# Attention: softmax inverses from a 128 by 16 layout, laid out and spread by transfers

## The chip, the cores and the metric

The kernel runs on one core of a Trainium2 chip. Its matrix engine (PE), vector engine (DVE), scalar engine (ACT) and general engine (POOL) each work through a program of their own and meet at semaphores; transfers are issued here by a fifth sequencer (SP). The metric is the time of one execution on the device in microseconds (us). Before the change the median of three runs is 5288.91 us.

## The reference

The program is one transformer block over x of shape (4, 2048, 512), in float32: a layer norm, then 16 heads of attention and a mixture of two experts beside each other, both added to x. What matters here is the attention:

```python
qkv = jnp.einsum('bnc,dc->bnd', x, qkv_w) + qkv_b
q, k, v = (qkv[0], qkv[1], qkv[2])        # each (4, 16 heads, 2048, 32)
attn = jnp.einsum('bhqd,bhkd->bhqk', q, k) * scale
attn = jax.nn.softmax(attn, axis=-1)
out = jnp.einsum('bhqk,bhkd->bhqd', attn, v)
...
x = x + _L0_attn_ref(xn, ...) + _L0_ffn_ref(xn, ...)
```

The softmax needs the largest score of each row, the exponentials, their sum, and a division by the sum. The kernel divides at the end: it multiplies the finished products of exponentials and values by the inverse of the sum.

## The kernel before

There are three stages one after the other: `dense_stage` (norm, projections, experts, to about 1,310 us of the profile), `attention_stage` (to 5,087 us) and `output_stage`. The change is in the second.

**Groups.** Attention is cut into 64 groups: 4 batches by 4 sets of four heads, each by 4 chunks of 512 queries. The four chunks of one set of heads share their keys and values. A group holds, for four heads and 512 queries, all 2048 keys. Eight groups (two sets of heads) make one turn of a loop; the first and the last turn are written out, six run in the loop.

**Units and scores.** PE computes each group's scores twice. The first time, one group ahead, it makes 64 *units* of 128 by 512 scores in three banks `mx_ps` (L890), and DVE takes the maxima of each (L829): unit n may only be written once the maxima of unit n-3 are taken. The second time (L951), with the maxima already folded in as one more row, the scores go to `st_ps`, and ACT takes the exponential into `p_sb` (L814). POOL adds the exponentials in pairs (L766, L756). PE multiplies them by the values (L902, sum in `o_ps`) and adds the pairs up with a matrix of ones (L910, sum in `sum_ps`). Those ones are 32 columns wide, so in `sum_ps` all 32 partitions of a head hold the same 512 sums.

**The order of the work** is written by hand. A group has 8 steps; the strings `STEPS` (L645) say what PE does in each: U is a unit, S a block of scores, V the products with the values, Z the sums, T the transposed maxima. Most steps read `USUSUSV...USUSUSUSUS`: three units, the products, then five more units. Of one step, `units_of(j)` lists the units, and DVE walks the same list (L861 to L873).

**The inverses.** They belong to the group before. In step 1 of a group ACT copies the finished sums of the group before to `sum_raw` (L792, 128 partitions by 512). DVE inverts them in 8 pieces of 64 columns (L843), two in each of the steps 2 to 5: one after the third unit of a step (i == 2), which is just ahead of V on PE, the other after the seventh (i == 6), in the middle of the run of units. In step 6 it multiplies (L849, `normalise`), and SP stores the result (L696).

**SP's order.** At the start of a set of heads (qc == 0) SP issues the transfers of the next set's keys (three of 1 MB, L675) and values (1 MB, L679), and then three of 256 KB of queries (L683). In the other groups it issues three of queries alone. After that it waits for the shift of step 6 and stores the group before. Keys and values of a next set are loaded at the heads of 15 sets; at the first of them there are no inverses yet, so 14 groups (the 4th, 8th, ... 56th, counted from 0) have both.

Of the kernel before, what the change touches and what calls it, by code (L numbers as in the profile page):

```python
# [15 lines left out]
F32 = mybir.dt.float32  # L16
# [6 lines left out]
P = 128  # L23
B, N, C = 4, 2048, 512
H, D = 16, 32
# [4 lines left out]
TOK = 512  # L30
# [542 lines left out]
                turn(B - 1, True)  # L573


def attention_stage(nc, qh_d, ql_d, kh_d, kl_d, v_d, o_d):

# [3 lines left out]
    QC = N // TOK  # L583
    UN = 4 * TT * (N // 512)
    NP = KT // 2
    INV = 8
    SLOTS = 8
    AHEAD = 6
    SB = 3
# [10 lines left out]
    with ctx:  # L600
        def sb(name, shape, dt):
            return ctx.enter_context(nc.sbuf_tensor(name, shape, dt))

        def sem(name):
            return ctx.enter_context(nc.semaphore(name))
# [11 lines left out]
        o_raw = sb("o_raw", [P, TOK], F32)  # L617
        sum_raw = sb("sum_raw", [P, TOK], F32)
        o_inv = sb("o_inv", [P, TOK], F32)
        st_ps = [ctx.enter_context(nc.psum_tensor(f"st_ps{i}", [P, TOK], F32)) for i in range(SB)]  # L620
        mx_ps = [ctx.enter_context(nc.psum_tensor(f"mx_ps{i}", [P, 512], F32)) for i in range(3)]
        o_ps = ctx.enter_context(nc.psum_tensor("o_ps", [P, TOK], F32))
# [10 lines left out]
        exp_done, o_copied, sum_copied, shift_done = sem("exp_done"), sem("o_copied"), sem("sum_copied"), sem("shift_done")  # L633
        unit_done, max_done, inv_done, o_done = sem("unit_done"), sem("max_done"), sem("inv_done"), sem("o_done")
        pair_done = sem("pair_done")

        G = 2 * QC
        TURNS = NQ // 2
# [30 lines left out]
        with nc.Block() as block:  # L669

            @block.sync
            def _(sp):
# [13 lines left out]
                def load_shift(count, qc):  # L686
# [2 lines left out]
                    sp.dma_start(q_x[qc][R:R + 1, :, :].bitcast(F32),  # L689
                                 shift[:, :].bitcast(F32)).then_inc(shift_ld, 16)  # L690

                def store_group(turn0, it, qc, count):
                    dst = o_d[it, :, qc * TOK:(qc + 1) * TOK]
                    sp.lower_val(dst.offset * 4)
                    sp.wait_ge(o_done, count)
                    sp.dma_start(dst, o_inv[:, :]).then_inc(o_st, 16)  # L696
# [11 lines left out]
                def turn(L, first, last):  # L708
                    for g in range(G):
                        u, qc = g // QC, g % QC  # L710
                        it, more = L * 2 + u, not (last and u == 1)
                        if qc == 0 and more:

                            sp.wait_ge(pv_done, L * G * KT + g * KT)
                            load_keys(it + 1 if isinstance(it, int) else it + 1, 1 - u)
                            load_values(it + 1, 1 - u)
                        if qc > 0 and more:

                            sp.wait_ge(st_ready, L * G * SK + g * SK)
                            load_queries(it + 1, qc - 1)  # L720
                        if qc == 0 and not (first and u == 0):
                            sp.wait_ge(st_ready, L * G * SK + g * SK)
                            load_queries(it, QC - 1)
                        if not (last and g == G - 1):
                            load_shift(L * G + g + 2, (qc + 1) % QC)
                        if not (first and g == 0):
                            store_group(L, it - 1 if qc == 0 else it, (qc - 1) % QC, L * G + g)

                turn(0, True, False)
                with sp.Fori(1, TURNS - 1) as L:  # L730
                    turn(L, False, False)
                turn(TURNS - 1, False, True)
                store_group(0, NQ - 1, QC - 1, NQ * QC)
                sp.wait_ge(o_st, NQ * QC * 16)

# [38 lines left out]
            def _(act):  # L774
# [13 lines left out]
                def copy_sum(count):  # L788

                    act.wait_ge(sum_done, count * NS)  # L790
                    act.wait_ge(inv_done, (count - 1) * INV)
                    act.activation(sum_raw[:, :], sum_ps[:, :], ACT.Copy).then_inc(sum_copied, 1)  # L792

                turn_shift(1)
# [30 lines left out]
            def _(dve):  # L825
# [8 lines left out]
                    dve.wait_ge(rows_ready, count - 1)  # L834
                    dve.reduce_max(row_max[:, :], unit_max[:, :, :], AX.X).then_inc(max_done, 1)

                def invert(count, part):

                    cols = slice(part * TOK // INV, (part + 1) * TOK // INV)
                    if part == 0:  # L840
                        dve.wait_ge(sum_copied, count)
                        dve.wait_ge(o_st, (count - 1) * 16)
                    dve.reciprocal(o_inv[:, cols], sum_raw[:, cols]).then_inc(inv_done, 1)  # L843

                def normalise(count):

                    dve.wait_ge(inv_done, count * INV)
                    dve.wait_ge(o_copied, count)
                    dve.tensor_tensor(o_inv[:, :], o_raw[:, :], o_inv[:, :], ALU.mult).then_inc(o_done, 1)  # L849

# [8 lines left out]
                def turn(L, first, last):  # L859
                    for g in range(G):  # L860
                        for j in range(NP):  # L861
# [3 lines left out]
                            for i, n in enumerate(units_of(j)):  # L865
                                if not (last and g + ahead >= G):
                                    if n == 0:
                                        dve.wait_ge(max_done, L * G + g + 2)
                                    unit((L * G + g + ahead) * UN, n)
                                if 2 <= j < 6 and i in (2, 6) and not (first and g == 0):  # L870
                                    invert(L * G + g, 2 * (j - 2) + (i == 6))
                            if j == AHEAD - 1 and not (last and g + ahead >= G):
                                rows((L * G + g + ahead) * UN, L * G + g + 2)  # L873

# [1 line left out]
                with dve.Fori(1, TURNS - 1) as L:  # L876
                    turn(L, False, False)
                turn(TURNS - 1, False, True)
                for part in range(INV):
                    invert(NQ * QC, part)  # L880
                normalise(NQ * QC)

            @block.tensor
# [253 lines left out]
def block_kernel(nc, x, qkv_wT, qk_bT, v_b, proj_wT, proj_b, wr, br, w1, b1T, w2, b2, out):  # L1137
# [8 lines left out]
    xf = x.rearrange("b n c -> (b n) c")  # L1146
    of = out.rearrange("b n c -> (b n) c")
    dense_stage(nc, xf, x0, qkv_wT, qk_bT, v_b, wr, br, w1, b1T, w2, b2, proj_b, qh_d, ql_d, kh_d, kl_d, v_d, y_d)
    attention_stage(nc, qh_d, ql_d, kh_d, kl_d, v_d, o_d)
    output_stage(nc, proj_wT, o_d, y_d, of)  # L1150


# [28 lines left out]
```

## Time and profile before

| what | us |
|---|---|
| median of 3 runs (5285.81 to 5292.80) | 5288.91 |
| the profiled execution | 5284.76 |
| its span | 5281.8 |
| PE busy (matmuls) | 5093.4 |
| DVE busy | 3277.4 |
| ACT busy | 2587.7 |
| POOL busy | 3229.5 |
| reciprocals of 64 columns (L843), 512 of them | 276.2 |
| maxima (L829), 4096 of them | 2503.2 |

The span is the time between the first and the last instruction; the 3.0 us around it are start and end. Ends of matmuls are modelled, so PE counts as busy where it waits for less than the modelled length of its last matmul: its waits are better read from the distance between starts. The rows further down are from the views of this one profiled execution. Group 28 (counted from 0) stands for a group at the head of a set of heads inside the loop's turn, group 32 for one at the head of the turn.

### The profile page before, as it was taken

To read this page: it belongs to the slowest core of one execution; us is meant where nothing else is said; L and a number is where in the kernel's file an instruction comes from. 1 tells how busy PE (TensorE), PEld (TensorE's weight loads), DVE (VectorE), ACT (ScalarE), POOL (GpSimd) and SP (SyncE) were. 2 spreads that over 40 slices of the span, in tenths; PEclk is the share of its full clock that TensorE was granted. 3 is DMA by queue.
4 is the path that set the end of the run, shared out by engine and by line. 5 is a ranking of instruction groups with operands and counts; after the bars stand their busy time and mean duration, and the time that the engine had idled before them with its cause. 6 is when DMAs were issued, how large, how long until landed. Compare 5 with 4: busy or idle time off the path is not lost. (4 is left out here: it accounts for less than half of the span.)

```text
span 5281.8 us, 83204 instructions
## 1 busy us (share of the span) xinstructions
PE 5093.4 (96%) x25932; PEld 2867.8 (54%) x25932; DVE 3277.4 (62%) x5616; ACT 2587.7 (49%) x4717; POOL 3229.5 (61%) x861
## 2 busy tenths in 40 slices
PE   8999999999899999999999999999999999999979
PEld 6878878787444444444444444444444444444447
DVE  4232232331777777777777777777777777777724
ACT  2121121211366666666656666665666566666631
POOL 1212212122488788778877877887788778778830
PEclk9999999999799999999999999999999999999989
DMA  5343343432402112120202202020220202020047
GB/s 172 91 150 105 99 148 94 140 119 77 95 17 51 28 44 49 25 49 17 51 23 50 49 20 55 17 50 18 55 49 19 55 17 49 19 55 17 7 154 240
DMA packets 186069, 348.49 MB, mean 66 GB/s; under 512 B 17956, under 2 KB 51748, under 8 KB 177448
## 3 DMA queue, kind: packets, MB, share of 16 engines
q1 hardware_dynamic: 185640, 342.99, 23.2%
q8 instruction: 242, 3.96, 0.3%
q14 instruction: 187, 1.53, 0.1%
HBM read 208.19 MB, written 134.22 MB: 65 GB/s over the span
## 5 line engine op out<-in xcount | busy, mean ns | idle before, releaser
L829 DVE TENSOR_REDUCE unit_max<-mx_ps 128x1 f32<-128x512 f32 x4096 | 2503.2, 679 | 918.4 <-PE mx_ps L890 918.4
L766 POOL TENSOR_TENSOR p_pair<-p_sb 128x2048 f32<-128x2048 f32 x512 | 2366.0, 4637 | 781.2 <-PE sum_ps L910 418.3
L814 ACT ACTIVATE p_sb<-st_ps 128x512 f32<-128x512 f32 x4096 | 2212.9, 600 | 1041.4 <-PE st_ps L951 1031.2
L890 PE MATMUL mx_ps<-k_x,q_x 96*128 96x512 f32 x4096 | 1853.6, 461 | 100.6 <-DVE unit_max L829 49.4
L951 PE MATMUL st_ps<-q_x,k_x 97*128 97x512 f32 x4096 | 1629.2, 403 | 8.2 <-ACT p_sb L814 2.3
L890 PEld LDWEIGHTS mx_ps<-k_x,q_x 96*128 96x128 f32 x4096 | 767.5, 190 | 1162.6 <-DVE unit_max L829 836.9
L902 PE MATMUL o_ps<-p_sb,v_sb 128*32 128x512 f32 x8192 | 992.5, 602 | 0.0
L951 PEld LDWEIGHTS st_ps<-q_x,k_x 97*128 97x128 f32 x4096 | 777.6, 190 | 137.1 <-ACT p_sb L814 64.6
L756 POOL TENSOR_TENSOR p_pair<-p_pair 128x2048 f32<-128x2048 f32 x128 | 584.6, 4567 | 10.0
L285 POOL TENSOR_TENSOR h_lo<-h_f,h_hi 128x512 fp32r<-128x512 f32 x128 | 165.1, 1290 | 689.8 <-DVE h_hi L469 689.8
L902 PEld LDWEIGHTS o_ps<-p_sb,v_sb 128*32 128x32 f32 x8192 | 214.6, 109 | 490.8 <-issue 278.9
L342 ACT ACTIVATE h_f<-rot,b_sb 128x512 f32<-128x512 f32 x128 | 88.2, 689 | 644.5 <-PE rot L505 644.4
L910 PE MATMUL sum_ps<-p_pair,ones 128*32 128x512 f32 x3072 | 388.8, 593 | 4.8 <-POOL p_pair L766 4.7
L469 DVE CAST h_hi<-h_f 128x512 fp32r<-128x512 f32 x128 | 55.0, 431 | 542.2 <-ACT h_f L342 542.2
L843 DVE RECIPROCAL o_inv<-sum_raw 128x64 f32<-128x64 f32 x512 | 276.2, 542 | 66.5 <-ACT sum_raw L792 66.5
L326 ACT ACTIVATE qk_hi<-rot,qk_bias 128x512 fp32r<-128x512 f32 x128 | 88.1, 689 | 379.2 <-DMA q_lo_d<-qk_lo 167.2
L910 PEld LDWEIGHTS sum_ps<-p_pair,ones 128*32 128x32 f32 x3072 | 99.8, 110 | 237.8 <-issue 215.6
L503 PE MATMUL rot<-xnT_hi,wq_hi 128*128 128x512 f32 x512 | 202.1, 395 | 19.5 <-DVE qk_lo L433 11.4
L503 PE MATMUL acc<-we_hi,h_hi 128*128 128x512 f32 x512 | 206.1, 402 | 6.5 <-POOL h_lo L285 4.9
L503 PE MATMUL rot<-xnT_hi,we_hi 128*128 128x512 f32 x512 | 199.6, 390 | 1.6 <-DVE v_out L455 1.6
L504 PE MATMUL rot<-xnT_lo,wq_hi 128*128 128x512 f32 x512 | 201.1, 393 | 0.0
L505 PE MATMUL rot<-xnT_hi,wq_lo 128*128 128x512 f32 x512 | 201.1, 393 | 0.0
(92 smaller groups left out, 3513.4 us busy)
## 6 DMA issues: line engine op xcount, KB each, us to landing
q_x<-q_hi_d SPq DMA_DIRECT2D x128, 256.0 KB, 5.4
k_x<-k_hi_d SPq DMA_DIRECT2D x30, 1024.0 KB, 9.6
xt<-x SPq DMA_DIRECT2D x64, 256.0 KB, 2.7
stage<-w SPq DMA_DIRECT2D x32, 512.0 KB, 5.1
q_hi_d<-qk_hi SPq DMA_DIRECT2D x64, 256.0 KB, 3.0
q_lo_d<-qk_lo SPq DMA_DIRECT2D x64, 256.0 KB, 3.7
k_hi_d<-qk_hi SPq DMA_DIRECT2D x64, 256.0 KB, 2.6
k_lo_d<-qk_lo SPq DMA_DIRECT2D x64, 256.0 KB, 3.3
```

The costliest lines, as they stand in the source:

```text
L503: pe.matmul(out, lh, rh, start=start and k == 0, stop=False)
L504: pe.matmul(out, lh, rl, start=False, stop=False)
L505: op = pe.matmul(out, ll, rh, start=False, stop=stop and k == len(pairs) - 1)
L756: pool.tensor_tensor(p_pair[:, slot, :, :], p_pair[:, 0, :, :], p_pair[:, slot, :, :], ALU.add).then_inc(pair_done, 1)
L766: pool.tensor_tensor(p_pair[:, slot, :, :], p_sb[:, 2 * i % SLOTS, :, :], p_sb[:, (2 * i + 1) % SLOTS, :, :], ALU.add).then_inc(pair_done, 1)
L814: act.activation(p_sb[:, kt % SLOTS, h, :], st_ps[bank(g, m)][:, :], ACT.Exp, scale=SCALE).then_inc(exp_done, 1)
L829: dve.reduce_max(unit_max[:, n // 4, n % 4:n % 4 + 1], mx_ps[n % 3][:, :], AX.X).then_inc(unit_done, 1)
L843: dve.reciprocal(o_inv[:, cols], sum_raw[:, cols]).then_inc(inv_done, 1)
L890: pe.matmul(mx_ps[n % 3][:, :], q_x[qc][0:R, h, t * P:(t + 1) * P], k_x[u][0:R, h, kc * 512:(kc + 1) * 512], start=True, stop=True).then_i ...
L902: op = pe.matmul(o_ps[rows, :], v_sb[u][:, kt, rows], p_sb[:, kt % SLOTS, h, :], start=(kt == 0), stop=(kt == KT - 1))
L910: op = pe.matmul(sum_ps[h * D:(h + 1) * D, :], ones[:, :], p_pair[:, slot, h, :], start=(i == 0), stop=(i == NS - 1))
L951: pe.matmul(st_ps[bank(g, m)][:, :], k_x[u][:, h, kt * P:(kt + 1) * P], q_x[qc][:, h, :], start=True, stop=True).then_inc(st_ready, 1)
```

## The change

The sums are inverted in another shape. Since 32 partitions hold the same values, SP now takes one partition of each head, 4 by 512 sums, and lays them out as 128 partitions by 16 columns in `sum_t` (one transfer of 8 KB). DVE inverts that in one instruction, in step 3 after the third unit. SP writes the inverses to a scratch tensor `inv_d` in memory (8 KB), waits until they have landed, and reads them back with four transfers that copy each head's 512 inverses to its 32 partitions of `o_inv` (64 KB each). `normalise` is where it was and now waits for the four transfers. ACT's next copy of sums waits for the first transfer instead of for the reciprocals.

```diff
+                def spread_inverse(count):
+                    sp.wait_ge(sum_copied, count)
+                    sp.dma_start(sum_t[:, :], sum_raw[0:P:D, :]).then_inc(sum_ld, 16)
+                    sp.wait_ge(inv_done, count)
+                    sp.dma_start(inv_d.rearrange("h (r n) -> (h r) n", n=QR), inv_t[:, :]).then_inc(inv_st, 16)
+                    sp.wait_ge(inv_st, count * 16)
+                    if not (isinstance(count, int) and count == 1):
+                        sp.wait_ge(o_st, (count - 1) * 16)
+                    for h in range(4):
+                        sp.dma_start(o_inv[h * D:(h + 1) * D, :], inv_d[h, :].partition_broadcast(D)).then_inc(inv_ld, 16)
...
                         if qc == 0 and not (first and u == 0):
                             sp.wait_ge(st_ready, L * G * SK + g * SK)
                             load_queries(it, QC - 1)
+                        if not (first and g == 0):
+                            spread_inverse(L * G + g)
                         if not (last and g == G - 1):
                             load_shift(L * G + g + 2, (qc + 1) % QC)
...
                 turn(TURNS - 1, False, True)
+                spread_inverse(NQ * QC)
                 store_group(0, NQ - 1, QC - 1, NQ * QC)
...
-                    act.wait_ge(inv_done, (count - 1) * INV)
+                    if not (isinstance(count, int) and count == 1):
+                        act.wait_ge(sum_ld, (count - 1) * 16)
...
-                def invert(count, part):
-                    cols = slice(part * TOK // INV, (part + 1) * TOK // INV)
-                    if part == 0:
-                        dve.wait_ge(sum_copied, count)
-                        dve.wait_ge(o_st, (count - 1) * 16)
-                    dve.reciprocal(o_inv[:, cols], sum_raw[:, cols]).then_inc(inv_done, 1)
+                def invert(count):
+                    dve.wait_ge(sum_ld, count * 16)
+                    if not (isinstance(count, int) and count == 1):
+                        dve.wait_ge(inv_st, (count - 1) * 16)
+                    dve.reciprocal(inv_t[:, :], sum_t[:, :]).then_inc(inv_done, 1)
...
-                    dve.wait_ge(inv_done, count * INV)
+                    dve.wait_ge(inv_ld, count * 64)
...
-                                if 2 <= j < 6 and i in (2, 6) and not (first and g == 0):
-                                    invert(L * G + g, 2 * (j - 2) + (i == 6))
+                                if j == 3 and i == 2 and not (first and g == 0):
+                                    invert(L * G + g)
```

On DVE, the first group that has inverses (group 1) read like this before, from the maxima ahead of the first reciprocal to those of the row maxima:

```order
L829 TENSOR_REDUCE unit_max<-mx_ps 128x1 x33
L843 RECIPROCAL o_inv<-sum_raw 128x64
L829 TENSOR_REDUCE unit_max<-mx_ps 128x1 x4
L843 RECIPROCAL o_inv<-sum_raw 128x64
L829 TENSOR_REDUCE unit_max<-mx_ps 128x1 x4
L843 RECIPROCAL o_inv<-sum_raw 128x64
L829 TENSOR_REDUCE unit_max<-mx_ps 128x1 x4
L843 RECIPROCAL o_inv<-sum_raw 128x64
L829 TENSOR_REDUCE unit_max<-mx_ps 128x1 x4
```

Each group now has one reciprocal among its 64 maxima:

```order
L848 TENSOR_REDUCE unit_max<-mx_ps 128x1 x41
L861 RECIPROCAL inv_t<-sum_t 128x16
L848 TENSOR_REDUCE unit_max<-mx_ps 128x1 x23
L854 TENSOR_REDUCE row_max<-unit_max 128x16
L867 TENSOR_TENSOR o_inv<-o_raw,o_inv 128x512
```

It stands where the third of the eight stood; the other seven are gone. On SP, at the head of the second set of heads of the first turn (group 4), the order before is keys, values, queries, shift, store:

```order
L675 DMA k_x<-k_hi_d 32x4x2048 x2
L675 DMA k_x<-k_lo_d 32x4x2048
L679 DMA v_sb<-v_d 128x2048
L683 DMA q_x<-q_hi_d 32x4x512
L683 DMA q_x<-q_lo_d 32x4x512
L683 DMA q_x<-q_hi_d 32x4x512
L689 DMA q_x<-shift 1x16x128
L696 DMA o_d<-o_inv 128x512
```

Now the six new transfers stand between the queries and the shift, the first of them behind the 4.75 MB of keys, values and queries:

```order
L678 DMA k_x<-k_hi_d 32x4x2048 x2
L678 DMA k_x<-k_lo_d 32x4x2048
L682 DMA v_sb<-v_d 128x2048
L686 DMA q_x<-q_hi_d 32x4x512
L686 DMA q_x<-q_lo_d 32x4x512
L686 DMA q_x<-q_hi_d 32x4x512
L698 DMA sum_t<-sum_raw 128x1x16
L700 DMA inv_d<-inv_t 128x16
L705 DMA o_inv<-inv_d 32x512 x4
L692 DMA q_x<-shift 1x16x128
L711 DMA o_d<-o_inv 128x512
```

## Rows read from the trace of the kernel before

**Rows 1.** The page, engines: busy us (share of the span), instructions.

```profile
PE 5093.4 (96%) x25932; PEld 2867.8 (54%) x25932; DVE 3277.4 (62%) x5616; ACT 2587.7 (49%) x4717; POOL 3229.5 (61%) x861
```

**Rows 2.** Waits of PE between 1480 and 5010 us: total, times, longest.

```profile
PE mx_ps L890 <- DVE unit_max L829: 48.6, 183, 0.3
```

**Rows 3.** Group of instructions, 1480 to 5010 us: busy us, mean ns, idle before.

```profile
L829 DVE TENSOR_REDUCE unit_max<-mx_ps 128x1 f32<-128x512 f32 x3904 | 2386.5, 679 | 877.7 <-PE mx_ps L890 877.7
```

**Rows 4.** Timeline of PE, products with values, group 0: start us, us.

```profile
1395.12 1.92 PE L902 MATMUL o_ps<-p_sb,v_sb 128*32 128x512 f32 x16
1401.31 1.92 PE L902 MATMUL o_ps<-p_sb,v_sb 128*32 128x512 f32 x16
1407.51 1.92 PE L902 MATMUL o_ps<-p_sb,v_sb 128*32 128x512 f32 x16
1415.15 1.92 PE L902 MATMUL o_ps<-p_sb,v_sb 128*32 128x512 f32 x16
```

**Rows 5.** The same four of group 1.

```profile
1451.35 1.92 PE L902 MATMUL o_ps<-p_sb,v_sb 128*32 128x512 f32 x16
1457.95 1.92 PE L902 MATMUL o_ps<-p_sb,v_sb 128*32 128x512 f32 x16
1464.55 1.92 PE L902 MATMUL o_ps<-p_sb,v_sb 128*32 128x512 f32 x16
1472.60 1.92 PE L902 MATMUL o_ps<-p_sb,v_sb 128*32 128x512 f32 x16
```

**Rows 6.** Timeline of PE, units of group 28 around a reciprocal.

```profile
3015.90 0.50 PE L890 MATMUL mx_ps<-k_x,q_x 96*128 96x512 f32 x1
...
3016.90 0.50 PE L890 MATMUL mx_ps<-k_x,q_x 96*128 96x512 f32 x1 [0.27 <-DVE unit_max L829]
```

**Rows 7.** Timeline of DVE, group 28, steps 2 and 3.

```profile
3015.76 0.54 DVE L843 RECIPROCAL o_inv<-sum_raw 128x64 f32<-128x64 f32 x1
3016.22 2.42 DVE L829 TENSOR_REDUCE unit_max<-mx_ps 128x1 f32<-128x512 f32 x4
3018.55 0.54 DVE L843 RECIPROCAL o_inv<-sum_raw 128x64 f32<-128x64 f32 x1
3019.96 2.48 DVE L829 TENSOR_REDUCE unit_max<-mx_ps 128x1 f32<-128x512 f32 x4 [0.86 <-PE mx_ps L890]
```

**Rows 8.** Timelines of group 28: ACT's copy of the sums, SP's last queries.

```profile
3006.83 0.60 ACT L792 ACTIVATE sum_raw<-sum_ps 128x512 f32<-128x512 f32 x1 [2.22 <-PE sum_ps L910]
3002.10 0.38 SPq L683 DMA_DIRECT2D q_x<-q_hi_d  x1
```

**Rows 9.** Transfers issued 3001.9 to 3002.6 us: count, KB, us to landing.

```profile
q_x<-q_hi_d SPq DMA_DIRECT2D x1, 256.0 KB, 21.4
```

**Rows 10.** Group 32: last queries' issue, their us to landing, DVE's maxima.

```profile
3236.68 0.38 SPq L683 DMA_DIRECT2D q_x<-q_hi_d  x1
q_x<-q_hi_d SPq DMA_DIRECT2D x1, 256.0 KB, 19.8
3254.46 2.48 DVE L829 TENSOR_REDUCE unit_max<-mx_ps 128x1 f32<-128x512 f32 x4 [0.86 <-PE mx_ps L890]
```

**Rows 11.** The page, transfers: count, KB, median us to landing.

```profile
q_x<-q_hi_d SPq DMA_DIRECT2D x128, 256.0 KB, 5.4
```

**Rows 12.** All transfers, small and near ones: count, KB, us to landing.

```profile
o_d<-o_inv SPq DMA_DIRECT2D x64, 256.0 KB, 2.5
q_x<-shift SPq DMA_DIRECT2D x64, 8.0 KB, 1.8
b_sb<-b1T SPq DMA_DIRECT2D x8, 2.0 KB, 1.6
```

**Rows 13.** Windows of group 28: length, busy by engine, PEclk, DMA share, GB/s.

```profile
3021.00:3023.00 2.00, 2.00 (x9) 1.04 (x7) 2.00 (x5) 2.00 (x5) 2.00 (x1) 1.00 0.16 43
```

**Rows 14.** The end of attention: DVE's timeline.

```profile
5080.04 3.43 DVE L843 RECIPROCAL o_inv<-sum_raw 128x64 f32<-128x64 f32 x8 [42.84 <-ACT sum_raw L792]
5083.51 0.69 DVE L849 TENSOR_TENSOR o_inv<-o_raw,o_inv 128x512 f32<-128x512 f32 x1
```

More of the change, by code:

```diff
@@ L573, in _, with attention_stage @@
                 turn(B - 1, True)
-def attention_stage(nc, qh_d, ql_d, kh_d, kl_d, v_d, o_d):
+def attention_stage(nc, qh_d, ql_d, kh_d, kl_d, v_d, inv_d, o_d):
     R = 3 * D
@@ L585, in attention_stage @@
     NP = KT // 2
-    INV = 8
+    QR = 4 * TOK // P
     SLOTS = 8
@@ L619, in attention_stage @@
         o_inv = sb("o_inv", [P, TOK], F32)
+        sum_t = sb("sum_t", [P, QR], F32)
+        inv_t = sb("inv_t", [P, QR], F32)
         st_ps = [ctx.enter_context(nc.psum_tensor(f"st_ps{i}", [P, TOK], F32)) for i in range(SB)]
@@ L635, in attention_stage @@
         pair_done = sem("pair_done")
+        sum_ld, inv_st, inv_ld = sem("sum_ld"), sem("inv_st"), sem("inv_ld")
         G = 2 * QC
@@ L878, in _ @@
                 turn(TURNS - 1, False, True)
-                for part in range(INV):
-                    invert(NQ * QC, part)
+                invert(NQ * QC)
                 normalise(NQ * QC)
@@ L1148, in block_kernel @@
     dense_stage(nc, xf, x0, qkv_wT, qk_bT, v_b, wr, br, w1, b1T, w2, b2, proj_b, qh_d, ql_d, kh_d, kl_d, v_d, y_d)
-    attention_stage(nc, qh_d, ql_d, kh_d, kl_d, v_d, o_d)
+    inv_d = scratch("inv_d", (4, TOK))
+    attention_stage(nc, qh_d, ql_d, kh_d, kl_d, v_d, inv_d, o_d)
     output_stage(nc, proj_wT, o_d, y_d, of)
```

## The prediction

> **What bounds the kernel now.** I read the page first: PE is busy for 96% of the span, DVE for 62% [rows 1]. By that alone, work taken off DVE would be worth nothing. The waits of PE in the middle of attention say otherwise: 183 times PE was idle before a unit until DVE had taken a maximum, 0.27 us or a little less each, and 183 is three times the 61 groups of that stretch [rows 2]. So something on DVE reaches PE three times a group. The timelines show what. Among the maxima DVE sits at a pace of 0.60 us ((2.48 - 0.68) / 3, with the 0.68 us of one maximum [rows 3, 7]), and PE's units follow DVE's pace there, since only three banks lie between them. Where a reciprocal comes in the middle of the run (3015.76), the next maximum starts 0.46 us later, and PE's units, at 3015.90 and 3016.90, stand 1.00 us apart instead of 0.60 [rows 6, 7]: PE loses 0.40 us. Where a reciprocal comes just ahead of the products with the values (3018.55), DVE waits another 0.86 us for PE after it [rows 7]: this one is hidden under products that keep PE 1.92 us [rows 4].
>
> The kernel has its own control. In group 0 there are no inverses yet. Its products of steps 2 to 5 start 6.19, 6.20 and 7.64 us apart; those of group 1, with two reciprocals a step, 6.60, 6.60 and 8.05 us [rows 4, 5]. That is 20.03 us against 21.25: 1.22 us per group, in three portions of 0.4 us. It fits the three waits a group; the fourth reciprocal of that kind, in step 5, has only two units left behind it and costs nothing.
>
> **The change, part by part.** *The eight reciprocals go.* Groups 1 to 62 have units beside their inverses (group 63 has none left), so this gives back 62 x 1.22 = 75.6 us. The other half of the reciprocals gives nothing. The 0.46 us a maximum that DVE loses behind one of 64 columns bounds the new one of 16 columns between 0.1 (a quarter of it) and 0.46 us; I take 0.2, since most of it scales with columns: eight in a row take 3.43 us [rows 14], 0.42 each for 64 columns. It stands ahead of the products, under the same 0.86 us, and costs nothing by itself. POOL and ACT do the same as before.
>
> *A wait of DVE on a transfer comes in.* Behind it in DVE's program stand all further maxima, and PE stops three units later. How late can the sums land? In most groups early: ACT's copy ends 0.60 us after 3006.83 [rows 8], and a small transfer takes 1.6 to 1.8 us, one of 256 KB out of the chip's own memory 2.5 [rows 12]; landed by about 3010, with DVE there at 3018.1. In those groups the chain behind it also fits: reciprocal, 2 us to memory, 1.3 us to issue four transfers, 2 us back, some 6 us, ahead of a multiplication twenty microseconds after 3018; SP has nothing else to issue until then.
>
> At the 14 heads of sets with keys and values it is different. The three transfers of queries are issued behind 4 MB of them: the last, issued at 3002.10, lands 21.4 us later, at 3023.5, where the median of such a transfer is 5.4 [rows 8, 9, 11]. So they stood in line, and the new transfer, issued at about 3007.5, joins the line behind them. DVE is free 0.41 us earlier than before (one portion of 0.4 is saved ahead of it), and would go on with maxima at 3019.96 - 0.41 = 3019.55 [rows 7]. With the sums at 3023.5, 0.1 us to wake and 0.2 for the reciprocal it goes on at 3023.8: 4.26 us late. In group 32, at the head of a turn, the last queries land at 3236.68 + 19.84 = 3256.5, and DVE would go on at 3254.46 - 0.41 = 3254.05 [rows 10]: 3256.52 + 0.3 is 2.77 us later. The 14 are seven of each kind, which differ little among themselves: 7 x 4.26 + 7 x 2.77 = 49.2 us. All of it reaches PE, as the run that follows goes at DVE's pace and nothing in later steps is slack enough to win it back.
>
> The transfer's own share comes on top, behind the last queries. Bounds: as much as 1.6 to 2.5 us, a whole small transfer end to end [rows 12], if nothing of it overlaps; or less than nothing. From 3021 to 3023 the 16 DMA engines are busy for a share of 0.16, two or three of them, with the rest of the queries [rows 13]: if the sums travel only on engines that are done, they land 1.4 us before 3023.5, which in the seven groups of that kind would make 10 us less. I take 0.5 us: 7.0 us for the 14, 56.2 in all.
>
> The Trainium skill has a rule on just this (DMA: Bandwidth & Descriptors, "Why a DMA increments its semaphore by 16 and not by 1"): a transfer is split over the largest number of engines up to 16 that divides the slowest dimension of both sides. By it the sums, 4 rows on one side, would go over 4 engines with 32 pieces each, and not over 16. No row of before shows a transfer of that shape. By this rule the late engines of a group like 28 need not be among the four; if they are not, the 10 us above come off and a profiled run takes 5260, and if they are, each has four times the pieces and the share is nearer to the upper bound. The first lies in the forecast's own range below, the second leads to the rival of a later landing.
>
> *The end.* After the last group nothing covers the chain. Before, the multiplication starts 3.47 us after the copied sums (5080.04 to 5083.51 [rows 14]). Now: 2.0 for the sums to land, 0.2 for the reciprocal, 2.0 to memory, 1.3 until the fourth transfer is issued, 2.2 to its landing, 0.3 for wakes: 8.0 us. That is 4.5 us more on the path, with 3 and 6.5 as bounds if each of the three legs takes 1.6 or 2.5 us [rows 12].
>
> *Sum*: -75.6 + 56.2 + 4.5 = -14.9 us. The profiled execution took 5284.8 us (span 5281.8 and 3.0 around it), so a profiled one should take 5270; the median of the runs is 4.1 us above the profiled one, so I forecast 5274 us for it, 0.28% faster. Most of what DVE gives back is lost again in 14 of 62 groups.
>
> **The rivals.** *The small transfer overtakes.* If it is served beside the big ones instead of behind them, DVE never waits in the heads: -75.6 + 4.5 = -71 us, 5218. For it speaks that pieces of 64 bytes are tiny; against it the queries, themselves a sixteenth of what is ahead, that waited 20 us.
>
> *The sums land later than that, and the kernel gets slower.* Break-even is where 14 delays eat 71.1 us: 5.08 us each, against the 4.0 I have on average. It decides from 1.1 us more. The mechanism would be the transfer's own latency at the end of the line: if 2.5 us and not 0.5 lie between the landing of the last queries and that of the sums [rows 12], the delays cost 28 us more and the time is 5302. For it: the pieces are small and many, and both ends lie in the chip's own memory, a pair of ends that the rows before never show. Against: the queries ahead, issued 0.4 us apart, do not each add a whole latency.
>
> *The reciprocals were never paid for*, and the two groups differ for another reason (group 0 also has no copies of sums on ACT). Then -75.6 is nothing and DVE's stalls remain: 5289 + 56 + 4.5 = 5349. The three waits a group stand against it.
>
> **How the numbers follow.** The forecast, with its own range of 5260 to 5288 (delays between 3.0 and 5.0 us), gets 0.62; overtaking or much of it 0.14; later landing 0.21; unpaid reciprocals 0.03. What a measurement of this kernel can tell from no change is about 0.2%, 10.6 us, so faster means below 5278.3 and slower above 5299.5. Of the forecast's 0.62, 0.40 lies below 5278 and 0.22 within; overtaking is all faster; of the later landing 0.06 is within and 0.15 slower; the last is slower. Faster 0.54, same 0.28, slower 0.18. The range of 8 in 10 takes in the later landing but not all of the overtaking: 5248 to 5303.
>
> **What would show it.** In the profile after: 62 groups without the three waits; products of steps 2 to 5 at 6.2, 6.2 and 7.65 us in ordinary groups; in 14 groups one distance of 6.2 plus 3 to 5 us between the products of steps 3 and 4, with DVE's reciprocal at the end of that wait and the sums' transfer landing 15 to 17 us after its issue instead of 2; the multiplication at the end some 8 us after the copy. Wrong would be: reciprocals in the heads that start at once, a landing over 2 us behind the last queries, or distances that stay at 6.6 us.

## The result, and the profile after

| | us |
|---|---|
| after, median of 4 runs (5320.62 to 5332.74) | 5328.92 |
| before, in the same rounds (5285.81 to 5292.80) | 5289.35 |
| ratio, 95% interval | 1.0073, 1.0055 to 1.0090 |
| profiled execution, after (before 5284.76) | 5330.07 |
| its span (before 5281.8) | 5327.6 |
| its mean granted clock of PE (before 0.987) | 0.971 |

The change makes the kernel 0.73% slower. The forecast was 5274 us with a range of 5248 to 5303: direction and range were wrong.

Look first at what got better, the engines' row of the page after (busy us, share, instructions):

```profile
PE 5137.1 (96%) x25932; PEld 2902.8 (54%) x25932; DVE 3205.5 (60%) x5168; ACT 2586.7 (49%) x4717; POOL 3221.3 (60%) x861
```

Against [rows 1], DVE lost 72 us of work, and PE, with the same 25932 instructions, is busy 44 us longer. Longer matmuls of the same number mean a lower clock. The waits between 1480 and 5050 us (total, times, longest) tell where that begins:

```profile
DVE inv_t L861 <- DMA sum_t<-sum_raw: 60.5, 14, 5.4
PE mx_ps L907 <- DVE unit_max L848: 49.6, 28, 3.8
```

The 183 waits of a quarter of a microsecond [rows 2] are gone, as forecast. In their place stand 14 waits of DVE on the sums, 4.3 us each, one in each of the 14 heads of sets, and 28 waits of PE: two per head, where the forecast has one. (The 4.0 us of the forecast are another quantity, the delay of DVE's next maximum. It comes below.)

To see what each head costs, take the distances between the products with the values (L919 after). Group 1, an ordinary one (start us, us of one):

```profile
1451.76 1.93 PE L919 MATMUL o_ps<-p_sb,v_sb 128*32 128x512 f32 x16
1457.94 1.93 PE L919 MATMUL o_ps<-p_sb,v_sb 128*32 128x512 f32 x16
1464.13 1.92 PE L919 MATMUL o_ps<-p_sb,v_sb 128*32 128x512 f32 x16
1471.78 1.92 PE L919 MATMUL o_ps<-p_sb,v_sb 128*32 128x512 f32 x16
```

6.18, 6.19 and 7.65 us instead of 6.60, 6.60 and 8.05 [rows 5]: the 1.22 us a group are there. Group 28, a head, steps 3 to 6:

```profile
3034.72 1.92 PE L919 MATMUL o_ps<-p_sb,v_sb 128*32 128x512 f32 x16
3045.39 2.54 PE L919 MATMUL o_ps<-p_sb,v_sb 128*32 128x512 f32 x16
3053.65 1.92 PE L919 MATMUL o_ps<-p_sb,v_sb 128*32 128x512 f32 x16
3059.84 1.93 PE L919 MATMUL o_ps<-p_sb,v_sb 128*32 128x512 f32 x16
```

The first distance is 10.67 us instead of 6.19, 4.5 us more, close to what was forecast. But the next is 8.26 instead of 7.65, and the matmuls of the second row take 2.54 instead of 1.92 us. Adding these distances over all groups and setting them against those of before gives the ledger:

| part | after minus before, us |
|---|---|
| 42 ordinary groups, 1.22 each | -51.2 |
| 14 heads, the same gain, 1.22 each | -17.1 |
| 14 heads, from the products of step 3 to those of step 4 (where the wait is) | +62.5 |
| 14 heads, steps 4 to 5 | +11.6 |
| 14 heads, steps 6 to 7 and 7 to the next group | +40.8 |
| the 6 other groups with inverses | -5.7 |
| end of attention | +5.1 |
| start and last stage | -0.4 |
| sum (the spans differ by 45.8) | +45.6 |

So behind the step of the wait the heads cost another 52.3 us, 3.7 each (the aftermath), and that alone turns the sign. How it comes about can be followed in group 28. DVE's and PE's timelines at the end of the wait:

```profile
3039.97 0.25 DVE L861 RECIPROCAL inv_t<-sum_t 128x16 f32<-128x16 f32 x1 [4.17 <-DMA sum_t<-sum_raw]
3040.14 3.06 DVE L848 TENSOR_REDUCE unit_max<-mx_ps 128x1 f32<-128x512 f32 x5
```

```profile
3040.82 0.80 PE L907 MATMUL mx_ps<-k_x,q_x 96*128 96x512 f32 x1 [2.57 <-DVE unit_max L848]
...
3065.31 0.50 PE L907 MATMUL mx_ps<-k_x,q_x 96*128 96x512 f32 x1 [0.83 <-DVE unit_max L848]
```

PE stood for 2.57 us and starts again with a unit of 0.80 us where 0.50 is usual: its clock has fallen. The windows of the group (length, busy by engine, granted clock, DMA share, GB/s) show it fall twice:

```profile
3034.70:3039.90 5.20, 3.55 (x23) 1.48 (x22) 1.10 (x2) 2.40 (x5) 5.12 (x2) 1.00 0.84 201
3039.90:3046.70 6.80, 5.88 (x18) 3.54 (x22) 5.31 (x9) 2.98 (x5) 5.87 (x2) 0.50 0.12 42
3046.70:3067.20 20.50, 19.37 (x104) 8.38 (x96) 16.59 (x22) 11.70 (x22) 15.66 (x5) 1.00 0.04 14
3067.20:3074.00 6.80, 6.80 (x26) 2.66 (x30) 2.95 (x5) 1.79 (x3) 4.18 (x1) 0.50 0.01 2
```

After the stop PE runs for 6.8 us at 1.2 GHz, then 20.5 us at 2.4 GHz, then 6.8 us more at 1.2 GHz. Over attention from 1480 to 5050 us there are 32 such stretches after: one at each of five loop back edges, 14 behind the waits, and in 13 heads a second one in step 6. Before there are 6: those of the back edges and one in group 62.

The first slow stretch begins at 3039.90, ahead of the products at 3045.39, so a part of the 62.5 us is slow clock and not wait. How much can be read from DVE. In group 1, whose products of step 3 start at 1457.94, it waits for PE before the next maximum although no transfer holds it:

```profile
1460.34 3.08 DVE L848 TENSOR_REDUCE unit_max<-mx_ps 128x1 f32<-128x512 f32 x5 [1.15 <-PE mx_ps L907]
```

This maximum starts 2.40 us behind the products of step 3; in group 28 it is 5.42 us (3034.72 to 3040.14). The delay is thus 3.0 us and not the 4.17 us of the wait: about 1.2 us of each wait lie where DVE would have waited for PE anyway. Over the 14 heads the delays make 44.4 us. The other 18 us of the 62.5 go with the slow stretch; e3 below has five heads without one, and there the step is longer by the delay alone.

Between the two slow stretches stands PE's other wait, of 0.83 us, and DVE and POOL tell what it is (DVE, then POOL):

```profile
3059.90 4.76 DVE L867 TENSOR_TENSOR o_inv<-o_raw,o_inv 128x512 f32<-128x512 f32 x1
3064.58 4.88 DVE L848 TENSOR_REDUCE unit_max<-mx_ps 128x1 f32<-128x512 f32 x8
```

```profile
3059.52 4.59 POOL L784 TENSOR_TENSOR p_pair<-p_sb 128x2048 f32<-128x2048 f32 x1 [1.95 <-ACT p_sb L833]
```

The multiplication, 0.69 us of work [rows 14], takes 4.76 us and ends 0.55 us after POOL's addition does. In an ordinary group it starts 2.7 us behind the start of an addition, and in the kernel before 4.1 to 4.4 us behind, when little of the 4.6 us is left. Here the stop and the slow stretch have moved it so late that it meets the next addition, which has also moved (POOL's own wait of 1.95 us on ACT) but less, and begins 0.38 us ahead of it. The maxima queued behind the multiplication are late, PE stops, and the clock falls again. Over all 64 groups (shortest, mean, longest, ns):

```profile
L867 DVE TENSOR_TENSOR o_inv<-o_raw,o_inv x64: 693/2435/4757, 1478.0 to 5130.1; 128x512 f32<-128x512 f32 x64
```

It is 2.4 us in most ordinary groups, where PE never waits for it, and 4.67 to 4.76 in each of the 14 heads. In both kernels 63 of the 64 multiplications start beside an addition, and each of them ends 0.55 or 0.56 us after that addition. Before, it took about 0.75 us in most groups:

```profile
3038.89 0.75 DVE L849 TENSOR_TENSOR o_inv<-o_raw,o_inv 128x512 f32<-128x512 f32 x1
```

The Trainium skill (SBUF — State Buffer, "Who interferes with whom") says that a DVE instruction with two inputs in SBUF, the on-chip memory, contends with a POOL instruction that reads SBUF, and that the shared ports are an exclusive lock. This trace agrees: 0.69 us of work took 4.76 us beside an addition of 4.59 us.

The end of attention after, SP's issues and DVE:

```profile
5123.21 0.58 SPq L698 DMA_DIRECT2D sum_t<-sum_raw  x1
...
5125.35 0.35 SPq L700 DMA_DIRECT2D inv_d<-inv_t  x1
...
5126.79 1.71 SPq L705 DMA_DIRECT2D o_inv<-inv_d  x4
```

```profile
5125.07 0.25 DVE L861 RECIPROCAL inv_t<-sum_t 128x16 f32<-128x16 f32 x1 [40.23 <-DMA sum_t<-sum_raw]
...
5130.08 0.69 DVE L867 TENSOR_TENSOR o_inv<-o_raw,o_inv 128x512 f32<-128x512 f32 x1 [4.75 <-DMA o_inv<-inv_d]
```

The copy of the sums ends at 5123.18. The multiplication starts 6.9 us later, against 3.47 [rows 14]: 3.4 us more where 4.5 were forecast. With nothing else on the queue the sums take 1.86 us from issue to reciprocal; in the heads 14.7 to 16.2.

### The profile page after: what moved, and what is told of

It reads as the page before. It is cut to its first block and busy times, and to the rows that moved or that the text cites. A ratio compares the mean times of both kernels' runs of the same rounds, so it can differ in the third digit from the quotient of the medians.

```text
span 5327.6 us, 83255 instructions
## 1 busy us (share of the span) xinstructions
PE 5137.1 (96%) x25932; PEld 2902.8 (54%) x25932; DVE 3205.5 (60%) x5168; ACT 2586.7 (49%) x4717; POOL 3221.3 (60%) x861
## 5 line engine op out<-in xcount | busy, mean ns | idle before, releaser
L907 PE MATMUL mx_ps<-k_x,q_x 96*128 96x512 f32 x4096 | 1875.0, 466 | 101.9 <-DVE unit_max L848 49.6
L968 PE MATMUL st_ps<-q_x,k_x 97*128 97x512 f32 x4096 | 1654.1, 409 | 8.4 <-ACT p_sb L833 2.3
L907 PEld LDWEIGHTS mx_ps<-k_x,q_x 96*128 96x128 f32 x4096 | 780.3, 193 | 1136.7 <-DVE unit_max L848 805.6
L919 PE MATMUL o_ps<-p_sb,v_sb 128*32 128x512 f32 x8192 | 1017.5, 615 | 0.0
L968 PEld LDWEIGHTS st_ps<-q_x,k_x 97*128 97x128 f32 x4096 | 791.9, 194 | 143.7 <-ACT p_sb L833 66.0
L919 PEld LDWEIGHTS o_ps<-p_sb,v_sb 128*32 128x32 f32 x8192 | 218.1, 111 | 513.8 <-ACT p_sb L833 273.6
L505 PE MATMUL acc<-we_hi,h_lo 128*128 128x512 f32 x512 | 200.6, 392 | 0.0
```

The source lines that it names most:

```text
L505: op = pe.matmul(out, ll, rh, start=False, stop=stop and k == len(pairs) - 1)
L907: pe.matmul(mx_ps[n % 3][:, :], q_x[qc][0:R, h, t * P:(t + 1) * P], k_x[u][0:R, h, kc * 512:(kc + 1) * 512], start=True, stop=True).then_i ...
L919: op = pe.matmul(o_ps[rows, :], v_sb[u][:, kt, rows], p_sb[:, kt % SLOTS, h, :], start=(kt == 0), stop=(kt == KT - 1))
L968: pe.matmul(st_ps[bank(g, m)][:, :], k_x[u][:, h, kt * P:(kt + 1) * P], q_x[qc][:, h, :], start=True, stop=True).then_inc(st_ready, 1)
```

## The experiments

The theory: in the heads the sums land late behind 4.75 MB, DVE stops, and PE pays for the stop three times (the stop, the slow stretch behind it, the multiplication locked behind POOL with a slow stretch of its own). The rivals: the reciprocals were never worth 75.6 us; or the transfers themselves disturb PE, DVE or POOL; or the 52 us belong to something else in the heads. Ratios are against the kernel before in the same rounds (5288.22 us in those of e1 to e4, 5298.48 us in those of e5 to e8, so times of the two sets are to be compared by ratio). "Excess" is the 14 heads' distances above 56.15 us, an ordinary group without reciprocals in the way.

### e1_four_pieces: the gain without the transfers

From the kernel before: four reciprocals of 128 columns, each just ahead of the products.

```diff
-    INV = 8
+    INV = 4
...
-                                if 2 <= j < 6 and i in (2, 6) and not (first and g == 0):
-                                    invert(L * G + g, 2 * (j - 2) + (i == 6))
+                                if 2 <= j < 6 and i == 2 and not (first and g == 0):
+                                    invert(L * G + g, j - 2)
```

> The kernel before, with four reciprocals of 128 columns instead of eight of 64, all in the place that was hidden (after the third unit of steps 2 to 5), none in the middle of a run of units. No transfers are added. Theory (the three mid-run reciprocals are what DVE's time was worth, and the lower clock of the changed kernel comes from its stalls): products of steps 2 to 5 at 6.2, 6.2, 7.65 us, 62 x 1.22 = 76 us less, 5213 us, and no more stretches at the lower clock than the kernel before has (11). Rival (a denser PE by itself makes the clock fall, as it fell in the changed kernel): stretches at 1.2 GHz in the heads of sets here too, and 5230 to 5265 us.

Measured: 5212.41 us, ratio 0.9851 (0.9834 to 0.9867), no excess. Among PE's own waits from 1480 to 5050 us none on DVE's maxima is left. DVE at the last reciprocal and the multiplication of group 27:

```profile
2945.03 0.94 DVE L843 RECIPROCAL o_inv<-sum_raw 128x128 f32<-128x128 f32 x1
2946.43 3.68 DVE L829 TENSOR_REDUCE unit_max<-mx_ps 128x1 f32<-128x512 f32 x6 [0.46 <-PE mx_ps L890]
2950.32 2.41 DVE L849 TENSOR_TENSOR o_inv<-o_raw,o_inv 128x512 f32<-128x512 f32 x1
```

After a reciprocal of 0.94 us DVE still waits 0.46 us for PE: it is hidden whole. The 75.6 us were real, and they came from the place of the reciprocals in the middle of the run of units (three of the four there, by the waits of [rows 2]), not from the work. This is the best version of all, faster than both kernels. It also shows that a multiplication of 2.4 us by itself costs nothing.

### e2_one_step_later: the same transfers, the reciprocal in step 4

```diff
-                                if j == 3 and i == 2 and not (first and g == 0):
+                                if j == 4 and i == 2 and not (first and g == 0):
```

> The changed kernel with one number different: the reciprocal stands after the third unit of step 4 instead of step 3, 7.6 to 8 us later. In the changed kernel the sums came 3.7 to 5.4 us too late in 14 groups. Theory (the wait in the 14 heads and what follows from it is the whole loss of 115 us): no wait on the sums anywhere, all ordinary and head groups at 56.2 us, 5329 - 115 = 5214, some 5217 us. Rival (the six transfers a group, their traffic and SP's longer program cost something by themselves): above 5235 us without such waits.

Measured: 5215.22 us, ratio 0.9856 (0.9839 to 0.9872). DVE waits for the sums in no head, the excess is 0, and of the slow stretches those at the five loop back edges are left, none in a head. All transfers are as in the changed kernel, so nothing of its loss belongs to them as such: all of it comes from DVE meeting the late sums. It is 2.8 us behind e1; that can't be told from nothing by these intervals, though the end's 3.4 us would be about it.

### e3_sum_on_act_queue: out of the line

ACT issues the sums' transfer from a queue of its own; SP keeps the rest.

```diff
-                    sp.wait_ge(sum_copied, count)
-                    sp.dma_start(sum_t[:, :], sum_raw[0:P:D, :]).then_inc(sum_ld, 16)
...
                     act.activation(sum_raw[:, :], sum_ps[:, :], ACT.Copy).then_inc(sum_copied, 1)
+                    act.wait_ge(sum_copied, count)
+                    act.dma_start(sum_t[:, :], sum_raw[0:P:D, :]).then_inc(sum_ld, 16)
```

> The changed kernel, with the transfer of the sums issued by ACT, on ACT's queue, right behind its copy; everything else stays on SP's. Theory (the sums are late because they stand behind the bulk in one queue): on a queue of their own they land in 2 to 5 us in the heads too, DVE does not wait, 5215 to 5230 us. Rival (the DMA engines are busy and any transfer started then is late): landing 15 us after its issue in the heads, waits of DVE as before, near 5329 us.

Measured: 5312.24 us, ratio 1.0039 (1.0025 to 1.0053), nearest to the rival's 5329, and as the rival had it, DVE got the sums 14.3 to 15.3 us after their issue. The excess is 84.4 us: 45.7 from step 3 to 4, 36.2 behind it, and 2.5 in step 1, where ACT now issues a transfer. DVE's waits:

```profile
DVE inv_t L861 <- DMA sum_t<-sum_raw: 52.3, 14, 4.3
```

3.7 us each instead of 4.3. So "the small transfer stands in line behind the big ones" is not the whole cause: it has hardly anything to gain from a line of its own. The page's row of that queue (packets, MB, share) and ACT's issue in the head shown:

```profile
q10 hardware_dynamic: 8448, 0.53, 0.1%
```

```profile
3022.85 0.56 ACTq L811 DMA_DIRECT2D sum_t<-sum_raw  x1
```

8448 packets for 64 transfers are 132 each: 128 pieces of 64 bytes and 4 packets of 4 bytes. The four fit the split over 4 engines that the forecast worked out; the records don't name a packet's engine. In this head the transfer was issued at 3022.85, and its pieces went out from 3029.6 to 3036.6 us, a few at a time, while the big transfers still ran (the last queries landed at 3038.4). DVE got them at last:

```profile
3037.68 0.25 DVE L861 RECIPROCAL inv_t<-sum_t 128x16 f32<-128x16 f32 x1 [3.84 <-DMA sum_t<-sum_raw]
```

So half of the 14.8 us pass while the pieces move. That they take turns with bulk packets is the likely reading, and e8 tests it; the 6.8 us until the first one moves are not explained by any run.

This run also parts the lock from the clock. In nine heads a slow stretch follows the wait. In the other five (groups 20, 24, 28, 44, 48) none does, and there the step of the wait is 2.06 to 2.64 us longer, with delays of DVE's next maximum of 2.11 to 2.69 us. Group 28: window, multiplication, PE's second wait.

```profile
3037.70:3063.00 25.30, 23.38 (x118) 10.40 (x119) 21.76 (x31) 14.56 (x27) 21.85 (x6) 1.00 0.08 23
```

```profile
3055.49 4.75 DVE L867 TENSOR_TENSOR o_inv<-o_raw,o_inv 128x512 f32<-128x512 f32 x1
```

```profile
3060.89 0.50 PE L907 MATMUL mx_ps<-k_x,q_x 96*128 96x512 f32 x1 [0.80 <-DVE unit_max L848]
```

The multiplication is locked all the same, at a granted clock of 1.00, so a shift of 2.1 us is enough for the lock and no slow stretch is needed. PE's second stop of 0.8 us costs 1.19 to 1.23 us in these five heads, and the clock doesn't fall behind it.

### e8_act_queue_64_pieces: half the pieces

As e3, with the sums laid out on 64 partitions by 32 columns.

```diff
-    QR = 4 * TOK // P
+    QR = 4 * TOK // 64
...
-        sum_t = sb("sum_t", [P, QR], F32)
-        inv_t = sb("inv_t", [P, QR], F32)
+        sum_t = sb("sum_t", [64, QR], F32)
+        inv_t = sb("inv_t", [64, QR], F32)
```

> As the run with the sums on ACT's queue (5312 us), but the sums laid on 64 partitions by 32 columns: 64 pieces of 128 bytes instead of 128 of 64. In that run the pieces of ACT's queue went out between 3029.5 and 3036.5, about one for each packet of the bulk on their four engines, and DVE waited 3.8 us. Theory (queues take turns piece by piece, so the number of pieces sets the landing): the pieces need half as long, 3.5 us less, DVE waits 0 to 0.6 us, 5215 to 5235 us. Rival (the sums land when the bulk is done, whatever their number): waits of 3 to 4 us as before, 5312 us.

Measured: 5227.33 us, ratio 0.9869 (0.9852 to 0.9886).

```profile
DVE inv_t L861 <- DMA sum_t<-sum_raw: 22.0, 14, 2.4
```

```profile
q10 hardware_dynamic: 4352, 0.53, 0.1%
```

```profile
2993.95 0.34 DVE L861 RECIPROCAL inv_t<-sum_t 64x32 f32<-64x32 f32 x1 [2.38 <-DMA sum_t<-sum_raw]
```

68 packets a transfer instead of 132, and the wait falls from 3.7 to 1.6 us: the pieces matter, though less than in proportion (in the head shown they go out in 5.6 us instead of 7). The time is in the expected range, but the wait was expected to be 0 to 0.6 us. More telling is what these waits cost. 22 us of them, the longest 2.4, make an excess of only 8.6 us: no slow stretch follows any, and in no head does the multiplication take over 2.4 us. Of the excess 6.3 us lie in the step of the wait, so about 1.1 us of each wait are absorbed ((22.0 - 6.3) / 14), as in the kernel after, and the other 2.3 come from ACT's issue in step 1 (it adds some 0.14 us to each ordinary group too). The price per microsecond of wait is not constant.

### e4_no_multiplication: the second stop taken out

The kernel after, with a short reduction of one operand in place of the multiplication. It leaves out the normalisation, so its output is wrong and it serves for the timing alone.

```diff
-                    dve.tensor_tensor(o_inv[:, :], o_raw[:, :], o_inv[:, :], ALU.mult).then_inc(o_done, 1)
+                    dve.reduce_max(o_inv[:, 0:1], o_raw[:, 0:64], AX.X).then_inc(o_done, 1)
```

> The changed kernel, but DVE's multiplication of 128 by 512 (two inputs) is left out and a maximum over 64 columns (one input) stands in its place, with the same waits; the output is not normalised. In the changed kernel the multiplication takes 2.4 us in ordinary groups and 4.7 in heads instead of 0.75, as long as POOL's addition beside it still runs. Theory: that lock is a part of the loss: in the 14 heads the step behind it (27 us of excess in all) shrinks by 10 to 25 us, 5305 to 5320 us. Rival (that excess is the clock alone, falling again after the first stall): heads as before, 5329 us.

Measured: 5287.18 us, ratio 0.9996 (0.9986 to 1.0005). The waits of DVE and PE:

```profile
DVE inv_t L861 <- DMA sum_t<-sum_raw: 62.6, 14, 5.2
...
PE mx_ps L907 <- DVE unit_max L848: 40.4, 14, 3.6
```

DVE waits as long as ever, but PE stops 14 times and not 28, and no second slow stretch is left (19: five of the back edges, 14 behind the waits). The excess is 77.3 us: 61.8 in the step of the wait, 15.2 from step 4 to 5, nothing in steps 6 and 7, where the kernel after loses 40.8. In ordinary groups the multiplication costs nothing either way, so those 40.8 us are what it brings when it meets POOL's addition in a head. The run is 42 us faster than the kernel after, where 10 to 25 had been expected: the second slow stretch goes with the lock. By e3's price of 1.2 us a head the lock itself is some 17 of the 40.8 us and the second stretch some 24.

### e5_long_hold: a stop without any transfer

From e1: in the same 14 heads, in step 3, DVE executes eight extra reciprocals of 64 columns, each waiting for the one before, into a tensor nobody reads.

```diff
+                                    if j == 3 and g % 4 == 0 and not (last and g == 4):
+                                        for m in range(8):
+                                            if not (first and m == 0):
+                                                dve.wait_ge(held, L * 16 + (g // 4 - 1) * 8 + m)
+                                            dve.reciprocal(hold[:, :], sum_raw[:, 0:64]).then_inc(held, 1)
```

> The version with four hidden reciprocals (5212 us), and in the 14 heads DVE is held at the place of the changed kernel's wait (step 3, after the third unit) by eight more reciprocals of 64 columns, each waiting for the last, into a tile that nobody reads: some 4 to 4.5 us beyond what is hidden. No new transfers. Theory (a stop of DVE of that length is enough for the whole loss: PE at 1.2 GHz behind it, then the multiplication locked behind POOL's addition, then 1.2 GHz again): heads 7 to 8.5 us longer, 5212 + 105 to 120, near 5322 us. Rival (the aftermath belongs to the transfers that were in flight): only the hold itself, 5212 + 14 x 4.2 = 5271 us.

Measured: 5341.24 us, ratio 1.0080 (1.0062 to 1.0097). DVE in group 4:

```profile
1628.15 4.60 DVE L878 RECIPROCAL hold<-sum_raw 128x64 f32<-128x64 f32 x8
...
1652.70 4.67 DVE L851 TENSOR_TENSOR o_inv<-o_raw,o_inv 128x512 f32<-128x512 f32 x1
```

```profile
PE mx_ps L897 <- DVE unit_max L831: 60.9, 28, 3.5
```

PE's 28 waits are back, with no transfer of sums in the kernel. The excess is 129.8 us: 75.2 in the step of the hold (5.4 each, of which the delay of DVE's next maximum is 4.0 and the rest goes with the slow clock) and 54.6 behind it (12.5, 27.0 and 15.0 in the segments where the kernel after has 11.6, 27.1 and 13.7). The same aftermath from another cause of such a stop: it belongs to the stop, not to transfers.

### e6_short_hold: half the stop

The same with four reciprocals (`range(4)`, 2.25 us in all).

> The same with four held reciprocals instead of eight: about 2 us beyond what is hidden. If the aftermath is an answer to the length of PE's stop, little of it remains: 14 x 2 = 28 us, 5240 us. If any stop in that place brings the same aftermath (3.7 us a head), 5212 + 28 + 52 = 5292 us. If the lock of the multiplication depends on how far the two engines' phases have been shifted, a value between, with the multiplication at 2.4 to 4.7 us.

Measured: 5271.04 us, ratio 0.9954 (0.9940 to 0.9967); excess 62.8 us, 28.8 in the step of the hold and 34.0 behind it. This divides the heads, though PE's stop is the same in all 14 (1.16 to 1.19 us) and so is the delay of DVE's next maximum (1.6 us). In eight heads the clock falls behind the hold, their step is 2.06 to 2.82 us longer, and the multiplication is locked. In the other six it doesn't fall and the step is 1.53 to 1.58 us longer; in five of these (groups 8, 32, 36, 40, 48) nothing follows, and in group 24 the multiplication is locked even so and the clock falls behind that. The nine heads with a lock pay the 34.0 us, 3.8 each, as much as in e5. PE's waits number 23, 14 and 9 more:

```profile
PE mx_ps L897 <- DVE unit_max L831: 24.5, 23, 1.5
```

The multiplication of a head whose clock fell behind the hold (28), of one whose clock never fell (32), and of group 24, DVE's rows and POOL's beside them:

```profile
3041.67 4.70 DVE L851 TENSOR_TENSOR o_inv<-o_raw,o_inv 128x512 f32<-128x512 f32 x1
...
3277.33 0.85 DVE L851 TENSOR_TENSOR o_inv<-o_raw,o_inv 128x512 f32<-128x512 f32 x1
...
2809.80 5.38 DVE L851 TENSOR_TENSOR o_inv<-o_raw,o_inv 128x512 f32<-128x512 f32 x1
```

```profile
3041.24 4.58 POOL L768 TENSOR_TENSOR p_pair<-p_sb 128x2048 f32<-128x2048 f32 x1 [0.73 <-ACT p_sb L816]
...
3273.03 9.61 POOL L768 TENSOR_TENSOR p_pair<-p_sb 128x2048 f32<-128x2048 f32 x2
...
2805.49 9.14 POOL L768 TENSOR_TENSOR p_pair<-p_sb 128x2048 f32<-128x2048 f32 x2
```

In group 28 the addition begins 0.43 us ahead of the multiplication, which then takes 4.70 us. In group 32 the multiplication starts just before the end of one addition, gets in ahead of the next and takes 0.85 us; that next addition takes 5.04 us instead of 4.58. In group 24 it starts at the same place, but the next addition goes first with its 4.58 us, and the multiplication takes 5.38 us. So a delay of 1.6 us sits on the edge of the lock, and 2.1 us (e3) is past it. What follows the stop comes in lumps: nothing without a lock, 1.2 us for a lock at full clock (e3), 3.8 us for a lock and slow clock. Why the clock falls behind some of 14 equal stops and not behind others stays open.

### e7_long_hold_no_multiplication: both at once

e5 with the reduction of e4 in place of the multiplication.

```diff
-                    dve.tensor_tensor(o_inv[:, :], o_raw[:, :], o_inv[:, :], ALU.mult).then_inc(o_done, 1)
+                    dve.reduce_max(o_inv[:, 0:1], o_raw[:, 0:64], AX.X).then_inc(o_done, 1)
```

> The long hold, with the multiplication left out as in the earlier run (a maximum over 64 columns in its place; the output is not normalised). Theory (the second stop in step 6 comes from the lock alone, and the second fall of the clock from that stop): step 6 and 7 of the heads as in ordinary groups, excess left is the hold and the clock right behind it, 14 x 5.5 = 77 us, 5289 us. Rival (the second fall of the clock answers to the first stop): excess in steps 6 and 7 remains, above 5300 us.

Measured: 5298.68 us, ratio 1.0003 (0.9993 to 1.0013). PE's waits are 14 again:

```profile
PE mx_ps L897 <- DVE unit_max L831: 49.4, 14, 3.5
```

The excess is 86.4 us: 73.0 in the step of the hold, 13.4 from step 4 to 5, nothing later. Against e5, 43 us go with the multiplication. With e4 this settles the two parts of what follows the step of the stop: 11 to 15 us over 14 heads for the rest of the first slow stretch, some 40 us for the multiplication locked behind POOL and the stretch that follows it. The second fall of the clock needs the lock (without it none in e4 and e7), but the lock does not always bring it: of the heads with a lock it followed in 40 of 45 whose clock had fallen once already (after, e3, e5, e6), in none of e3's five whose clock had not, and in group 24 of e6, where PE's stop was the longest of these, 1.49 us.

## Why the prediction was wrong

- *The eight reciprocals go: -75.6 us.* Right. The ledger has -51.2 and -17.1 in the groups, and with those of the back edges and group 62 (-5.7) it is -74.0. e1 shows it alone: 75.8 us less than before.
- *The sums land late in 14 heads.* Right in place, too large in size. The forecast's 56.2 us are delays of DVE's next maximum; measured, these are 44.4 us. It put 4.76 us on the heads inside a turn and 3.27 on those at its start, and both have 3.2. The term of 0.5 us behind the last queries had the wrong sign: the sums landed 0.8 us ahead of them on average. That the step of the wait lost 62.5 us, near 56.2, is luck: some 18 us of slow clock filled the gap. The reason given was half right: a queue of its own wins only 0.6 us a head (e3). As far as its four packets of 4 bytes tell, the transfer travels on 4 engines and not on 16, as the Trainium skill's rule has it (DMA: Bandwidth & Descriptors, "Why a DMA increments its semaphore by 16 and not by 1"), 32 pieces on each, and with half the pieces the wait is 2.1 us shorter (e8).
- *"All of it reaches PE, as the run that follows goes at DVE's pace and nothing in later steps is slack enough to win it back."* This is the step that failed. It asks only whether something is won back, not whether more is lost: a stop was priced at the delay of DVE alone, and the slow clock and the lock behind it were put at nothing. The kernel after loses 70.5 us more than the delays (114.9 of excess less 44.4): some 18 within the step of the wait, 11.6 in the next, 40.8 in steps 6 and 7. e5 reproduces it with no transfer (54.6 us behind the step of the hold), e4 and e7 divide it in two.
- *"POOL and ACT do the same as before."* True of their work and wrong of their phase. The stop moved DVE's multiplication against POOL's additions in all 14 heads, and [rows 5] and the tail could not show that, since in the kernel before the multiplication came at the very end of an addition and lost 0.4 us at most by it.
- *The end: +4.5 us.* Measured 3.4 for the chain; the end of attention as a whole is 5.1 longer. Write and read back through memory were each a little faster than taken:

```profile
inv_d<-inv_t SPq DMA_DIRECT2D x64, 8.0 KB, 1.4
...
o_inv<-inv_d SPq DMA_DIRECT2D x256, 64.0 KB, 2.0
```

- *The sum.* Forecast -14.9, measured +45.3 in the profiled executions. Of the 60.2 us between, +70.5 are slow clock and lock, -11.8 the delays, +1.6 the gain, and the rest cancels. With the stops at the forecast's own price, their delay alone, the profiled time would by this ledger have been some 5260 us (5330.07 - 70.5), against the 5270 forecast for it.
- *The rivals.* The one on the slower side had the direction, but by a landing 2.5 us behind the last queries, 28 us more of delay. Against the last queries the sums landed earlier than forecast, and the delays were 11.8 us less. The price of a stop, not its length, decided.

The length was not safe the other way either: e8's 22 us of waits cost 8.6.

## What to carry to other kernels

A reciprocal, or any small instruction, costs by where it stands: three of eight places here cost 75 us and the others nothing, so move it under a wait of the same engine (e1) before replacing it. A wait added in front of an engine's queue is to be placed where its latest case, not its usual one, is covered; one step later, with no other change, was worth 2% (e2 against the kernel after). And where a stop does reach PE, add what follows it. Here that was 4.4 to 5.3 us on top of the delay for each stop that ended in a slow clock and a multiplication locked behind POOL, whether the delay was 1.6 us (e6) or 4.0 us (e5), and 1.2 us where the multiplication was locked at full clock (e3).

## What the runs showed of the hardware that was not expected

- PE's stops of 2.2 to 3.8 us (after, e4, e5, e7) were followed by 3.4 to 10.2 us of PE at 1.2 GHz in all 14 heads. Stops of 1.7 to 2.8 us were in 9 of 14 (e3), stops of 1.2 us in 8 of 14 (e6), and those of e8, at most 0.9 us, in none.
- A multiplication of 0.69 us took 4.67 to 4.76 us whenever an addition of POOL (4.6 us) had just begun, and it didn't slow that addition. An addition that came while the multiplication was already waiting for the one before took 5.04 us (e6, group 32).
- A transfer of 8 KB in 128 pieces of 64 bytes took 1.86 us until DVE used it with nothing else on the queue and 14.7 to 16.2 behind 4.75 MB; on a queue of its own it still took 14.3 to 15.3, and in 64 pieces 12.1 to 13.4.
